# Moving the setup of a graph transformer kernel: first input first, later stages' weights prepared inside the feed-forward stage

## What is computed

```python
# layer 0: transformer block, 8 heads of 32
normed = layernorm(x, g1, b1)
q, k, v = (normed @ W + b for W, b in ((Wq, bq), (Wk, bk), (Wv, bv)))
w = softmax(q k^T / sqrt(32) + 2*adj - 1) * (0.25 + 0.75*adj)
w = w / max(w.sum(-1), 1e-6)
hidden = x + (w v) @ Wo + bo
x = hidden + gelu(layernorm(hidden, g2, b2) @ Wf1 + bf1) @ Wf2 + bf2     # Wf1: 256x1024
# layer 1: two graph attentions, 8 heads and then 1 head
def gat(x, W, a_src, a_dst):
    h = x @ W;  s, t = h . a_src, h . a_dst          # per head
    return softmax(leaky_relu(s[:, None] + t[None, :], 0.2) + adj) h
x = x + gat(layernorm(x, lg1, lb1), W1, as1, ad1)
x = x + gat(layernorm(x, lg2, lb2), W2, as2, ad2)
```

## Time and profile before

| | |
|---|---|
| median of 3 runs | 1146.68 us |
| profiled execution | 1150.13 us, span 1148.3 us |
| TensorE busy | 1081.8 us (94% of the span) |
| VectorE, ScalarE, GpSimd busy | 776.5, 714.5, 404.9 us |
| chain that ended last | PE 81%, DVE 7%, issue 5%, POOL 3% |
| mean granted TensorE clock | 0.978 |
| stages, from the start of the span | setup and chunk 0 to 46.3 us, A to 432.6, B to about 798, C to about 985, D to the end |

### The profile page before, as it was taken

The page is one execution under the profiler, slowest core; times in us unless marked ns, Lnnn a source line. Parts: engine busy times, 40 slices in busy tenths (PEclk is TensorE's granted clock), DMA queues, the critical chain, the costliest instruction groups (busy, mean ns, idle before and its releaser), DMA issues.

```text
span 1148.3 us, 41349 instructions
## 1 busy us (share of the span) xinstructions
PE 1081.8 (94%) x16172; PEld 945.4 (82%) x16172; DVE 776.5 (68%) x1908; ACT 714.5 (62%) x1702; POOL 404.9 (35%) x628
## 2 busy tenths in 40 slices
PE   5799999999999989999999999998899999879997
PEld 4688888888888868899989988997788888767775
DVE  5677677776777774554455445545688898858886
ACT  2467777677776755553454355435788888656763
POOL 1541121111211103231123112321378788774542
PEclk9799999999999999999999999999899999989998
DMA  8021111011010000000000000000010000001212
GB/s 223 16 76 30 29 30 57 30 30 30 30 39 12 12 2 1 1 1 1 0 0 0 0 0 0 0 1 10 13 30 18 27 18 19 5 20 55 73 60 87
DMA packets 41737, 31.18 MB, mean 27 GB/s; under 512 B 5281, under 2 KB 41377, under 8 KB 41633
## 3 DMA queue, kind: packets, MB, share of 16 engines
q1 hardware_dynamic: 36736, 28.84, 8.0%
q10 hardware_dynamic: 4896, 0.80, 0.6%
HBM read 21.25 MB, written 8.39 MB: 26 GB/s over the span
## 4 chain that ended last, share of the span: by engine, by line
PE 81%; DVE 7%; issue 5%; POOL 3%; ACT 2%; DMA 1%; DVEq 1%; SPq 0%; POOLq 0%; ACTq 0%
PE BK L1313 6%; PE BK L1191 5%; PE BK L1190 5%; PE BK L1399 5%; PE BK L1397 5%; PE BK L1189 5%; PE BK L1398 5%; PE BK L1287 4%; PE BK L1299 4%; PE F L1189 3%; PE BK L1280 3%; PE F L1191 3%; PE F L1190 3%; PE F L1205 3%; PE BK L1456 3%
## 5 line engine op out<-in xcount | busy, mean ns | idle before, releaser
L1058 ACT ACTIVATE gf<-BK,bcol 128x512 f32<-128x512 f32 x128 | 88.0, 688 | 178.8 <-PE BK L1191 167.9
L852 POOL TENSOR_TENSOR ve<-mv,eps_l 128x4 f32<-128x4 f32 x64 | 13.6, 212 | 451.1 <-DVE mv L293 412.3
L977 ACT ACTIVATE e_sb<-BK,nmx 128x128 f32<-128x128 f32 x512 | 141.4, 402 | 28.5 <-DVE nmx L449 28.5
L1397 PE MATMUL BK<-wf_hi,gh 128*128 128x256 f32 x512 | 143.0, 279 | 0.0
L1398 PE MATMUL BK<-wf_hi,gl 128*128 128x256 f32 x512 | 141.6, 277 | 0.0
L1399 PE MATMUL BK<-wf_lo,gh 128*128 128x256 f32 x512 | 141.6, 276 | 0.0
L542 DVE TENSOR_TENSOR gl<-gf,gh 128x512 fp32r<-128x512 f32 x128 | 93.6, 732 | 64.4 <-ACT gh L1059 62.5
L455 DVE TENSOR_TENSOR pt_sb<-BK,ft 128x512 f32<-128x512 f32 x128 | 85.3, 687 | 67.4 <-PE BK L1287 66.1
L997 ACT ACTIVATE xn<-x_all,neg_mr,rstd 128x256 f32 (+1 forms) x188 | 102.9, 602 | 33.0 <-POOL neg_mr L861 29.5
L556 DVE TENSOR_TENSOR x_all<-BK,x_all 128x256 f32 (+1 forms) x64 | 27.2, 425 | 117.1 <-PE BK L1399 117.1
L1191 PE MATMUL BK<-xh,wf_lo 128*128 128x512 f32 x256 | 100.8, 394 | 0.0
(11 more groups left out here) (206 smaller groups left out, 2888.6 us busy)
## 6 DMA issues: line engine op xcount, KB each, us to landing
x_all<-in_x_dram SPq DMA_DIRECT2D x16, 512.0 KB, 4.2
adj_in<-in_adj_dram SPq DMA_DIRECT2D x32, 256.0 KB, 2.8
out_dram<-y SPq DMA_DIRECT2D x16, 512.0 KB, 2.9
s_wf<-in_L_gnn_Wf_dram SPq DMA_DIRECT2D x2, 1024.0 KB, 11.7
s_w<-in_L_gnn_W_dram SPq DMA_DIRECT2D x2, 256.0 KB, 8.4
s_wq<-in_L_gnn_Wq_dram SPq DMA_DIRECT2D x1, 256.0 KB, 3.5
s_wk<-in_L_gnn_Wk_dram SPq DMA_DIRECT2D x1, 256.0 KB, 4.3
s_wv<-in_L_gnn_Wv_dram SPq DMA_DIRECT2D x1, 256.0 KB, 4.6
```

What stands on the lines that cost most here:

```text
L977: e = act.activation(e_sb[:, j, :], LE[:, r, q, :], ACT.Exp, bias=nmx[:, j:j + 1], scale=1.0)
L1058: act.activation(gf[f % 2][:], BK[:, f % 4, :], ACT.Gelu, bias=bcol[:, 6 + f:7 + f])
L1397: pe.matmul(dst, gh[:, f, n], hi[:, f, :], start=(f == 0), stop=False)
```

## The change

SyncE now issues x and adj of chunk 0 first, then wq, wk, wv (own semaphore) and wo (another); wf1 and wf2 follow x and adj of chunk 1. w1, w2 and the four a vectors are loaded only when stage A is over, into memory that stage B leaves free. ScalarE issues the five vectors that the projections need first, with a semaphore of their own.

```diff
-            for w, name in ((wq, "wq"), (wk, "wk"), (wv, "wv"), (wo, "wo")):
-                sp.dma_start(stage[name][:], kp(w)).then_inc(w_in[0], 16)
...
                 if isinstance(i, int) and i == 0:
-                    sp.wait_ge(w_in[3], 16 * len(small_cols))
-                    for w, name in ((w1, "w1"), (w2, "w2")):
-                        sp.dma_start(stage[name][:], kp(w)).then_inc(w_in[2], 16)
+                    for w, name in ((wq, "wq"), (wk, "wk"), (wv, "wv")):
+                        sp.dma_start(stage[name][:], kp(w)).then_inc(w_qkv, 16)
+                    sp.dma_start(stage["wo"][:], kp(wo)).then_inc(w_out, 16)
+                if isinstance(i, int) and i == 1:
+                    sp.wait_ge(w_cols, 16 * len(first_cols))
                     for w, name in ((wf1, "wf1"), (wf2, "wf2")):
-                        sp.dma_start(stage[name][:], kp(w)).then_inc(w_in[1], 16)
+                        sp.dma_start(stage[name][:], kp(w)).then_inc(w_ff, 16)
...
+            gate(a_x, NG)
+            for w, name in ((w1, "w1"), (w2, "w2")):
+                sp.dma_start(stage[name][:], kp(w)).then_inc(w_l1, 16)
+            for n, a in enumerate((as1, ad1, as2, ad2)):
+                sp.dma_start(a_bc[n][:], a.rearrange("h k -> (h k)").partition_broadcast(P)).then_inc(w_l1, 16)
```

```diff
-                    if isinstance(i, int) and i == 1 and pp == 0:
-                        pe.wait_ge(setup_dve, setup_at["all"])
+                    if isinstance(i, int) and i == 1 and pp == 1:
+                        pe.wait_ge(setup_dve, setup_at["biases"])
...
                         ln_turn(i + CA)
+                        if first:
+                            setup_projections()
+                        if isinstance(i, int) and i == 1:
+                            setup_biases()
...
                             if first:
-                                pe.wait_ge(setup_dve, setup_at["projections"])
+                                pe.wait_ge(setup_dve, setup_at["splits"])
...
-                if first:
-                    setup_biases()
```

```diff
+                if isinstance(i, int) and i == 0:
+                    setup_marks()
+                if isinstance(i, int) and i == 1:
+                    setup_scores(0)
+                if isinstance(i, int) and i == NC - 4:
+                    setup_scores(1)
+            chunks(dve, b_step, tail=4)
...
+                    if first == CA and isinstance(i, int) and i == 1:
+                        setup_lo("wf1", False, 1)
+                        setup_lo("wf2", True, 2)
+                    if first == CB and isinstance(i, int) and i == 0:
+                        pool.wait_ge(w_l1, 16 * 6)
+                        setup_gain("w1", 24)
+                        setup_gain("w2", 28)
+                    if first == CB and isinstance(i, int) and i == 1:
+                        setup_lo("w1", False, 3)
+                        setup_lo("w2", False, 4)
```

```diff
+            def setup_constants():
+
+                pe.wait_ge(setup_dve, setup_at["scores"])
                 for layer, b_at in ((0, 22), (1, 26)):
+                    bias_column(F[1][:, layer:layer + 1], wc[:, layer], 0, b_at)
+                for n, name in enumerate(("w1", "w2")):
+                    r = broadcast_row(F[0][:, n * D:(n + 1) * D], lb_wide[n], name)
                 r.then_inc(setup_pe, 1)
...
                 pe.wait_ge(ln_xl, (i + CB) * KT + 2)
+                if isinstance(i, int) and i == NC - 3:
+                    setup_constants()
                 for f in range(FT):
                     wait_for(pe, b_gh, i * FT + (f - 3))
                     wide(BK[:, f % 4, :], "wf1", f * P).then_inc(b_h, 1)
+                if isinstance(i, int) and i == NC - 3:
+                    pe.wait_ge(setup_dve, setup_at["all"])
                 ln_turn(i + CB + 1)
```

More of the change, by code:

```diff
@@ L164, in build @@
         gf = [o(f"gf{r}", [P, W4]) for r in range(2)]
+        for name in ("w1", "w2"):
+            stage[name] = o(f"s_{name}", [P, KT, D])
+            scaled[name] = o(f"{name}_g", [P, KT, D])
+        a_bc = [o(f"a_bc{n}", [P, D]) for n in range(4)]
+        lb_wide = [o(f"lb_wide{n}", [P, KT, P]) for n in range(2)]
+        prod = o("prod", [P, KT, D])
+        wa = o("wa", [P, 2, 2, KT, H])
+        wag = o("wag", [P, 2, 2, KT, H])
+        wst = o("wst", [P, KT, P])
+        wc = o("wc", [P, 2, KT, P])
+        marks = o("marks", [P, 8])
         gt_all = overlay(at_wf1, at_wf1 + 4 * KT * FF * 4)("gt_all", [P, NG * P])
@@ L331, in split @@
                                                       in1=hi[:, kt, :].bitcast(F32), op0=ALU.mult, op1=ALU.subtract))
-            for n in range(2):
-                done(dve.memset(wst[:, n], 0.0))
-                done(dve.memset(wc[:, n], 0.0))
-                done(dve.memset(wa[:, n], 0.0))
             done(dve.memset(exp_bias[:], LOG_3_4 - 1.0))
@@ L424, in setup_rows @@
-                setup_at["rows"] = steps[0]
-            def setup_biases():
-                dve.wait_ge(setup_pe, 2)
-                done(dve.tensor_tensor(bo_bc[:], BK[:, 3, 0:D], bo_bc[:], ALU.add))
-                done(dve.tensor_tensor(bcol[:, 6:14], BK[:, 4, 6:14], cols[:, 14:22], ALU.add))
+                        done(dve.tensor_tensor(lo[:, :, D + side:D + side + 1], wag[:, 1, side, :, 0:1],
+                                               hi[:, :, D + side:D + side + 1].bitcast(F32), ALU.subtract))
@@ L431, in setup_biases @@
+                    setup_at["scores"] = steps[0]
+            def setup_constants():
+                dve.wait_ge(setup_pe, 3)
                 done(dve.tensor_scalar(cb[:], marks[:, 6:7], FACTOR_SHIFT, None, ALU.mult))
                 settle()
-                done(dve.scalar_tensor_tensor(out=cb[:], in0=BK[:, 4, 14:15], scalar=-0.8, in1=cb[:], op0=ALU.mult, op1=ALU.add))
-                done(dve.tensor_scalar(turn_const[:, 0:1], BK[:, 4, 15:16], 0.8, None, ALU.mult))
-                done(dve.tensor_copy(c1_bc[:], BK[:, 5, 0:D]))
@@ L436, in setup_biases @@
-                done(dve.tensor_copy(c2_bc[:], BK[:, 5, D:2 * D]))
+                done(dve.scalar_tensor_tensor(out=cb[:], in0=F[1][:, 0:1], scalar=-0.8, in1=cb[:], op0=ALU.mult, op1=ALU.add))
+                done(dve.tensor_scalar(turn_const[:, 0:1], F[1][:, 1:2], 0.8, None, ALU.mult))
+                done(dve.tensor_copy(c1_bc[:], F[0][:, 0:D]))
+                done(dve.tensor_copy(c2_bc[:], F[0][:, D:2 * D]))
                 setup_at["all"] = steps[0]
@@ L493, in a_step @@
                         a_max(sp, 0)
-                    if pp == 0:
+                    if pp == 0 and not first:
                         ln_lo(i + CA)
@@ L773, in a_step @@
                     load_a(i + 1, half + par, 1 - par)
[L774 to L778 removed]
+                if par == 1 and not (isinstance(i, int) and i == 1):
+                    sp.wait_ge(setup_dve, setup_at["biases"])
+                    sp.wait_ge(setup_act, 2)
+                    sp.wait_ge(setup_pool, 3)
                     sp.wait_ge(setup_pe, 2)
@@ L1025, in a_step @@
                         a_exps(sp, 3)
+                    if isinstance(i, int) and i == 1:
+                        if pp == 0:
+                            setup_hi("wf1", False, 1)
+                        else:
+                            setup_hi("wf2", True, 1)
                     if not tail:
@@ new lines, in broadcast_row @@
+            def broadcast_row(dst, wide_b, name):
+                for kt in range(KT):
+                    r = pe.matmul(dst, wide_b[:, kt, :], stage[name][:, kt, :],
+                                  start=(kt == 0), stop=(kt == KT - 1), skip_group_check=True)
+                return r
+            def setup_biases():
+                pe.wait_ge(setup_dve, setup_at["wide"])
+                pe.wait_ge(w_out, 16)
+                pe.wait_ge(w_ff, 32)
+                pe.wait_ge(w_late, 16 * (len(later_cols) + 2))
+                broadcast_row(BK[:, 5, 0:D], bv_wide, "wo")
```

239 lines of the change are left out of this document (114 added, 125 removed).

## The result

The changed kernel took 1155.04 us in the median of 20 runs (1150.75 to 1159.78), the kernel before 1150.82 us in 20 runs beside them (1146.65 to 1159.03). The ratio is 1.0041, interval 1.0028 to 1.0054, which is 4.7 us (the two medians alone lie 4.2 us apart). It is slower where 5.2 us less were forecast, and lies above the predicted range. Of the 13.5 us between the forecast 1141.5 and 1155.04, 4.1 are the starting point: the forecast began from the 1146.68 us of three runs, and in 20 runs the kernel before took 1150.82. The other 9.4 are the change. The profiled execution took 1156.84 us, its span 1155.0. One execution of e4 and one of the kernel before took 1727 and 1728 us, at a mean clock of 0.56, and are in no ratio.

What follows compares the result with a forecast made beforehand. TensorE was taken to bound the kernel from 46.3 us to the end of stage B. Stage A -16.7 and stage B +11.5 gave -5.2 us: 1144.9 from the profiled 1150.13, less 3.5 for the median, 1141.5; range 1135 to 1148.

Steps and rivals of the forecast that it cites:

- The step that failed: Stages C and D, doing the same work as before, were to change by 0 us.
- Stage B: Setup work moved into this stage's steps was to cost +11.5 us, between +6 and +16.
- step 13: Stage B, scores of w2 and constants: 4.3 us idle, 2.7 constants, 1.7 low clock, together 8.7 us.
- the two rows: Half-clock stretches after the setup's gap (10.0 us) and stage C's idle (3.0 us), used to size step 13's 1.7 us.
- The waits for `xn`: Stage B, early steps: 1.3 us from the scores of w1 and 1.5 us from GpSimd's products blocking VectorE.
- the rule: Trainium skill: certain VectorE and GpSimd instructions lock each other out in SBUF; `xn` blocking likely 3.0 us, not 1.5.
- Stage A: Was to change by -16.7 us, between -13 and -20: earlier start -2.6, gap -16.1, step 1 +2.0.
- Step 1: Stage A, first step after the gap: added work less removed waits makes it 2.0 us longer, between 0.5 and 5.
- the gap: Stage A, from projections' end to logits of chunk 1: 16.1 us in which no chunk advances, all to go.
- The slower case: Clock falls at each of five new TensorE waits, 14.4 us in place of 1.7: 1154.2 us, chance 0.07.
- Rival 4: Start not shortened because x of chunk 1 or wf1 queue behind weights: 1144.1 us; chance 0.55 together with the forecast.
- Rival 1: Stage B hides most of the added work, clock stays up in step 13: -10.7 us, 1136.0 us, chance 0.20.

Runs made afterwards that it cites:

- e4: The changed kernel with GpSimd's gains and lo parts of w1 and w2 put behind its bias additions in step 0 of stage B; ratio 1.0037 to the kernel before.
- e2: The changed kernel with two steps of stage B written out instead of four, scores of w2 and constants one step later; ratio 0.9994 to the kernel before.
- e10: The changed kernel with TensorE's last six steps of stage B written out instead of four; ratio 0.9979 to the kernel before.
- e3: The changed kernel with VectorE's marks and scores behind the first residual add of their step instead of the last; ratio 0.9972 to the kernel before.
- e1: The kernel before with TensorE's last four steps of stage B written out instead of two; ratio 1.0025 to the kernel before.
- e5: The changed kernel with the edits of e2, e3 and e4 together; ratio 0.9909 to the kernel before.
- e9: e5 with wf1's 32 one-column matmuls in four separated groups of 8 and ScalarE's table loaded earlier; 1134.7 us, ratio 0.9864 to the kernel before.
- e11: e9 with TensorE's last six steps of stage B written out instead of two; 1134.5 us, ratio 0.9867 to the kernel before.

## Why the prediction was wrong

**The step that failed** is the one line "Stages C and D do the same work; their weights are ready long before, their start has no new wait that ends late". The work is the same and the start has no new wait, and yet C took 6.8 us more. The prediction followed semaphores and engines only, and left out that a longer written-out tail moves every later instruction of TensorE. Of stage C's 6.8 us, 2.2 are waiting (the "issue" waits grew by 2.8) and 3.5 the half clock, which lasted 7 us longer; 1.1 are not assigned. Undone in e2 (with the constants one step later) and changed alone in e10, the tail gives back 0.5 and 0.6% of the time, 5 to 7 us. That is the larger part of the 9.9 us between the forecast difference (-5.2) and the measured one (+4.7). In the profiles, where -5.2 stands against +6.7, stage C has 6.8 us of the 11.9, B 3.3, A 1.5 and D 0.3. Without this step the forecast gain would still not have come, by the sizes below: e2, with two steps, only ties with the kernel before.

**Stage B** was seen rightly, and undersized by 3.3 us. The idle of step 13 came at 4.29 us (forecast 4.3). The step grew by 10.45 us where 8.7 were forecast: I had sized the low clock by the 3.0 us after stage C's idle, "since dense blocks follow". The constants come first, 8 one-column and 8 small matmuls that themselves ran at half clock (3.76 us for the eight of lb_wide, 1.97 in e3), and the clock stayed low for 6.7 us. Busy time at half clock costs half of itself, 3.4 us where 1.7 stood. The reason does not hold either: the same idle of 5.3 us at the start of stage C, with the same work behind it, was followed by 3.0 us at half clock in the kernel before, by 4.3 in e1 and by 5.8 in e4 and e10. And the other of the two rows was no case of idle time. In the kernel before the clock fell at 33.73 us, when the 32 one-column matmuls (30.22 to 33.85) were still running, ahead of the wait of 4.32 us:

```profile
30.22:33.73 3.51, 3.51 (x34) 3.51 (x32) 3.44 (x16) 0.00 (x0) 2.47 (x3) 1.00 0.08 22
33.73:33.85 0.12, 0.12 (x2) 0.03 (x1) 0.11 (x1) 0.00 (x0) 0.00 (x0) 0.51 0.00 0
```

That step 13's idle did bring the clock down (e3) agrees with the forecast, but of the two rows only one stood behind it. The waits for `xn` sum to 3.3 us against 1.3 + 1.5 = 2.8, and steps 0 to 3 grew by 4.3 us with them; this is the other 1.5 of the 3.3 us. Their forecast of "about 1 us in steps 0 to 2" holds: 0.71, 1.14, 1.41. Beside GpSimd's products `xn` grew by 1.4 and 1.9 us; less the slack of 0.7 twice, which was rightly read, that made waits of 1.85 us, between the 1.5 taken and the upper end of 3.0 that the rule would have made the likely one.

**Stage A** gave 14.5 to 15.2 us of 16.7. x first came true to 0.1 us: statistics at 5.39 (forecast 5.3). But the projections started at 18.52, not 17.9, since what I had left out lay on ScalarE. Its queue issues the vectors' DMAs until 12.24 us, two of them taking 3.30 us, loads its table at 12.27, and makes `xh` only at 13.68; VectorE's `xl` waits for that, and the splits behind it. The logits of chunk 1 stand at 29.16 against 27.7. 0.6 us of this is the later start; the other 0.9 is the clock, since chunk 0's projections took 10.64 us and 9.73 before. One of 0.63 us is at half clock, one of 0.39 at full, and the change from one to the other came near 23 us in both kernels (22.95 and 23.4), though TensorE began at 10.17 instead of 11.90. So what was won ahead of 23 us was spent in part at half clock. Step 1 grew by 1.1 us and the wait for `v` stands right behind it, 1.7 together and not 2.0, though by other terms: that wait is 0.56 us and not 1.3, and the low clock that I had struck out with the gap is there again (0.93 in both windows), with another cause. The gap went in full.

**The rivals.** The slower case was named, and its time of 1154.2 us was near the result, but by luck: it stood for +7.5 us over 1146.68, and +4.7 us over 1150.82 was measured, for another reason. It put the low clock at every new wait of TensorE, five places at 2.9 us. At the waits of 0.56 to 1.41 us no stretch at half clock was found; stage B as a whole has 0.99. The clock fell at one of these places (step 13) and at two that the rival did not have (behind the one-column matmuls and behind the first "issue" wait). Rival 4 is refuted by the logits at 29.16 and the missing gap. Rival 1, that B hides most, is what e3 to e5 made of it: once the scores lie in VectorE's slack, B costs 3.4 us more than before and the start's gain shows.

**What stays open.** What TensorE waits for in "issue" isn't measured. Nor is it shown why the clock falls behind such a wait in the changed kernel and not in e1. The profile adds up to +6.7 us and the times to +4.7; the scatter of one profile covers that.

## What to carry to other kernels

Work put into a busy stage is free only in the slack of the engine that does it. Ask which instruction it stands behind, and put it where the next consumer is latest: behind the first residual add instead of the last was worth 8.8 us of stage B. When a change alters how many steps are written out behind a loop, time that number by itself, two or three values of it, before the change is judged; here it turned a gain into a loss. And count the one-column matmuls that stand together, since they can cost the clock behind them although TensorE never waits.

## What the runs showed that was not expected

- The granted clock fell with no idle time of TensorE: to 0.50 to 0.52 from 36.9 us, right behind 32 one-column matmuls in 3.63 us. Two groups of 16 did not prevent it, four groups of 8 with other work between them did. In the eight profiles with one or two groups it fell between 34.9 and 38.1 us, for 3.4 us (6.8 in e3); in e9 and e11 it fell nowhere in stage A. Which property of these matmuls does it was not tried.
- The idle of 4.3 us ahead of the constants was followed by 5.7 to 6.8 us at half clock in the four kernels that have it, 1.94 us of "issue" by 6.6 us, and stage C's idle of 5.3 us, with the same work behind it, by 2.9 to 5.8 us in the thirteen profiles. Neither the length of the idle nor the work that follows gives the length of what comes.
- Stage C took 212.5 to 215.6 us in the three kernels of the changed form with four steps written out, 209.2 to 211.6 in the five with two, and 205.5 and 206.6 in the two with six.
- Two small loads took 3.30 us to issue on ScalarE's queue behind its others, while a load of x on SyncE's queue took 0.44.
